# A selective scan beside a GpSimd read-out: the read of a state waits for the next drive, and other VectorE work stands between scan and drive

## The reference

```python
x = x + attn_a(layernorm(x))   # linear attention: 16 heads of 8, features poly * exp of a projection, causal
x = x + ffn(layernorm(x))      # gate/up/down, 128 -> 352 -> 128, inputs and weights rounded to FP4 in blocks of 16
x = x + attn_b(layernorm(x))   # selective state-space mixer, below
x = x + ffn(layernorm(x))
```

```python
dA  = exp(dt[..., None] * A)                      # decay
dBu = (dt * u)[..., None] * B[:, :, None, :]      # drive
h   = dA_t * h + dBu_t                            # scan over the tokens
y   = einsum('bldn,bln->bld', hs, C) + u * D      # read-out: the state times C, summed over the 16 states
```

## Time and profile before

| | before |
|---|---|
| median of 3 runs | 1835.58 us (1835.45 to 1837.35) |
| the profiled execution | 1833.05 us |
| its span in the trace | 1831.2 us |
| mean granted TensorE clock | 0.809 |
| VectorE busy | 1478.3 us, 81% |
| TensorE matmul busy | 1198.0 us, 65% |
| ScalarE busy | 669.5 us, 37% |
| GpSimd busy | 644.6 us, 35% |
| DMA | 74.75 MB, mean 41 GB/s |

### The profile page before, as it was taken

The page is one execution under the profiler, slowest core; times in us unless marked ns, Lnnn a source line. Parts: engine busy times, 40 slices in busy tenths (PEclk is TensorE's granted clock), DMA queues, the critical chain, the costliest instruction groups (busy, mean ns, idle before and its releaser), DMA issues. The chain is left out here.

```text
span 1831.2 us, 14294 instructions
## 1 busy us (share of the span) xinstructions
PE 1198.0 (65%) x4361; PEld 659.3 (36%) x4361; DVE 1478.3 (81%) x1759; ACT 669.5 (37%) x1133; POOL 644.6 (35%) x420
## 2 busy tenths in 40 slices
PE   4967964786647864688647865478745884444554
PEld 1634522454224532355214542245422552221212
DVE  1745599887998789887998879987898879975974
ACT  2524532353324523264324533245232642223211
POOL 2012244423354133432444233541344223352531
PEclk9977977898769986799778987699877997775756
DMA  2000112010210111001210102101110011102210
GB/s 55 1 6 1 48 66 78 1 47 31 75 46 1 48 58 58 35 1 54 75 69 1 48 30 74 46 1 48 52 58 34 1 54 69 69 0 70 81 40 6
DMA packets 31405, 74.75 MB, mean 41 GB/s; under 512 B 4505, under 2 KB 14562, under 8 KB 31330
## 3 DMA queue, kind: packets, MB, share of 16 engines
q1 hardware_dynamic: 31330, 73.83, 11.7%
HBM read 71.20 MB, written 2.62 MB: 40 GB/s over the span
## 5 line engine op out<-in xcount | busy, mean ns | idle before, releaser
L554 POOL TENSOR_TENSOR read<-state,bc_row 128x1024 f32<-128x1024 f32 x128 | 316.3, 2471 | 457.9 <-DVE state L1022 443.6
L1011 DVE TENSOR_TENSOR bank<-dtu,bc_row 128x1024 f32<-128x1024 f32 x128 | 383.6, 2997 | 32.1 <-POOL dtu L634 19.6
L1289 PE MATMUL bank<-read,ident 128*128 128x512 f32 x512 | 330.2, 786 | 97.1 <-POOL read L554 97.1
L671 ACT ACTIVATE decay<-dt,neg_a 128x510 f32<-128x510 f32 x256 | 169.5, 711 | 353.4 <-DVE state L1022 352.3
L1022 DVE TENSOR_TENSOR_SCAN state<-decay,bank 128x1024 f32<-128x1024 f32 x128 | 291.5, 2277 | 4.2 <-ACT decay L671 0.5
L1289 PEld LDWEIGHTS bank<-read,ident 128*128 128x128 f32 x512 | 119.6, 251 | 244.4 <-POOL read L554 123.8
L1259 PE MATMUL bank<-s_sb,vext 128*72 128x256 f32 x512 | 168.3, 412 | 0.0
L1032 DVE TENSOR_TENSOR s_sb<-bank,causal 128x512 f32<-128x512 f32 x128 | 87.9, 687 | 94.1 <-PE bank L1242 93.3
L1240 PE MATMUL bank<-feat 64*128 64x256 f32 x512 | 109.8, 463 | 80.2 <-ACT s_sb L682 79.9
L1229 PE MATMUL bank<-znt,omega 128*128 128x512 f32 x256 | 141.2, 634 | 21.7 <-ACT sqf L662 21.6
L659 ACT ACTIVATE expf<-bank,minus_s,root2s 128x512 f32<-128x512 f32 x128 | 100.2, 783 | 129.0 <-PE bank L1229 128.7
(11 more groups left out here) (220 smaller groups left out, 2011.6 us busy)
## 6 DMA issues: line engine op xcount, KB each, us to landing
bc_row<-bc_rows SPq DMA_DIRECT2D x128, 512.0 KB, 3.6
xa<-x_dram SPq DMA_DIRECT2D x8, 256.0 KB, 2.8
out_dram<-x SPq DMA_DIRECT2D x8, 256.0 KB, 2.3
omega<-omega_t_dram SPq DMA_DIRECT2D x1, 512.0 KB
bc_rows<-xdbl SPq DMA_DIRECT2D x8, 64.0 KB
wqkv<-w_qkv_t_dram SPq DMA_DIRECT2D x1, 192.0 KB
state<-w_down_dram SPq DMA_DIRECT2D x1, 176.0 KB, 2.4
state<-w_gate_dram SPq DMA_DIRECT2D x1, 128.0 KB, 2.0
```

The costliest lines, as they stand in the source:

```text
L554: pool.tensor_tensor(read[:, s % STATE_BUFFERS], state[:, s % STATE_BUFFERS], bc_row[:, s % BC_BUFFERS, 1].unsqueeze(1).broadcast_to([P, D ...
L671: last = act.activation(decay[:, s % 2, k, :, 1:], dt[:, k].rearrange("p (b t) -> p b t", b=SEQS)[:, :, 1:], ACT.Exp, scale=neg_a[:, k, s: ...
L1011: dve.tensor_tensor(bank[:, DRIVE_BANK:DRIVE_BANK + DT], dtu[:], bc_row[:, s % BC_BUFFERS, 0].unsqueeze(1).broadcast_to([P, DT, TOK]), ALU ...
L1289: last = pe.matmul(bank[:, 6 + k], ident[:], read[:, s % STATE_BUFFERS, k], start=(s == 0), stop=(s == STATES - 1))
```

## The change

There are three edits. GpSimd's read_out(k) gets a second wait: for drive k+1 (in the last slot for all drives of the group). GpSimd's slot has `attention_rest(k)` ahead of read_out(k) instead of behind it. VectorE's slot is scan(k), `attention_rest(k)`, drive(k+1).

```diff
@@ read_out (GpSimd)
                 pool.wait_ge(state_done.sem, state_done.at(group, s + 1))
 
+                pool.wait_ge(drive_done.sem, drive_done.at(group, min(s + 2, STATES)))
+
                 pool.wait_ge(y_ps.sem, y_ps.at(group, max(s + 1 - STATE_BUFFERS, 0)))
@@ body (GpSimd)
                 for k in range(SLOTS):
+                    attention_rest(turn, k)
                     if turn.has_old:
                         read_out(turn.old, k)
-                    attention_rest(turn, k)
@@ body (VectorE)
                     if turn.has_old:
                         scan(turn.old, k)
-                        if k + 1 < SLOTS:
-                            drive(turn.old, k + 1)
                     if turn.has_mid and k == 0:
                         attention_out(turn.mid, SEQS - 1)
                     attention_rest(turn, k)
+                    if turn.has_old and k + 1 < SLOTS:
+                        drive(turn.old, k + 1)
```

## The result

| | before | after |
|---|---|---|
| median | 1835.69 us (1835.45 to 1837.35, 4 runs) | 1710.20 us (1709.62 to 1718.48, 4 runs) |
| the profiled execution | 1833.05 us | 1709.62 us |
| its span | 1831.2 us | 1707.8 us |
| mean granted TensorE clock | 0.809 | 0.835 |
| VectorE busy | 1478.3 us | 1269.0 us |

The ratio is 0.9325, with a 95% interval of 0.9296 to 0.9354: 125 us faster. The forecast was 1722 us, with a range of 1680 to 1765.

What follows compares the result with a forecast made beforehand. VectorE was taken to bound the scan stage. Six turns gaining 13.1 us each (78.6), turn 8 14.9 and turn 9 19.9 sum to 113.4 off 1833.05: 1719.6, with 2.5 for the median 1722 us, range 1680 to 1765.

Steps and rivals of the forecast that it cites:

- (a): VectorE's drives in the scan stage: most fall to 1.22 us, two still wait at 1.73; 26.8 us gained a turn.
- (b): Normalisations of slots 1 and 3 stand for late reads, plus some seven other tails of 0.1: 3.0 us lost a turn.
- (c): Slots 8 to 10: Newton steps between read(8) and read(9) delay VectorE 1.8 us where 1.27 is today; 0.5 lost.
- (d): Slot 14: VectorE waits for a down-projection queued on TensorE behind sum(12), whose read ends later; 5.1 us lost a turn.
- (e): End of scan stage: read(15) comes behind norm_o's rstd, its sum runs slower; 5.1 us lost, between 3.2 and 5.5.
- TensorE's queue matters less: Rival, chance 0.13: the slot 14 loss and 1.9 us of the boundary loss go; 1671 us, half of it 1696.
- more places wait: Rival, chance 0.13: other TensorE queue positions come late, or GpSimd wins the port against drives; about 40 us more, 1762.
- The bound only changes its name: Rival, chance 0.03: saved drive time comes back as waits for decay or for a bc_row; 1835 us.
- Scan and read exclude each other: Rival, chance 0.04, the slower case: every scan of 15 waits 2.26 us for the read beside it; 1934 us.

## Why the prediction was right, point by point

The total was put 12 us too high. The mechanism held, and so did each of the places; the sizes:

**(a) Drives: right.** Forecast 26.8 us a turn. Twelve drives went from 3.41 to about 1.23 and two from 2.00 to 1.60 (forecast 1.73): 27.0. The open question, a drive 0.16 us ahead of scale_hidden, came out as taken: the first keeps what both need, drive 1.23, L539 2.59. Had it gone the other way, 27 us would have been lost by the forecast's own estimate; of the rows before the change, a single one, of another pair of instructions, spoke for this side. The two halves tried alone and the drive in SBUF show that the cause is the one named: the collision, and a scan that doesn't take part in it because one input lies in PSUM.

**(b) Tails: too high.** Forecast 3.0 lost. The normalisations of slots 1 and 3 took 2.01 and 2.99 where they took 1.10 and 2.05: 1.9. The seven tails of 0.1 don't show; slots with work gain the same 2.2 us as the bare one. This is the larger part of the 1.0 us by which the mean stage, 95.3 us, is shorter than forecast.

**(c) Slots 8 to 10: right.** Forecast 0.5 lost, slot 10 lost 0.4; VectorE waits 1.67 before qk (forecast 1.8) and qk takes 3.42. Undoing it gave 8 us in all.

**(d) Slot 14: right.** Forecast 5.1. The wait before L992 grew by 85.1 - 41.9 = 43.2 us, 5.4 for each of eight turns (in turn 9 it is in slot 8). It varies from turn to turn: slot 14 takes 8.7 to 10.1 in turns 2 to 7. In turn 4, the longest of them, the down-projection too ran at the low clock, 2.67 us where the forecast had 1.5. The turned queue took 32 us of it away.

**(e) The boundary: right in size.** Forecast 5.1, the rest grew by 5.2 in the mean, and the first mask comes 12.6 us behind the last scan instead of 7.4, also 5.2. The order of GpSimd undone brought it back to where it was, though the rest became only 1.6 us shorter, because of the new loss at the end of the stage. By parts in turn 4: the read ends 5.46 us behind the scan (forecast 5.6), the sum takes 3.31 (forecast 3.6), the projection 1.43 instead of 1.02. In turn 8 it cost 2.7, not 4.0.

**The sum.** Six turns gained 14.0 each (forecast 13.1), turn 8 16.1 (14.9), turn 9 20.1 (19.9); that is 7 of the 10 us by which the gain in the span, 123.4, exceeds 113.4. The other 2.8 lie behind turn 9's last scan, which the forecast left alone: 57.6 us before, 54.8 after, with the same work at a granted clock of 0.71 instead of 0.62. The last 2 us are the median's: after's lies 0.6 above its profiled execution, not 2.5.

**The rivals.** *TensorE's queue matters less* and *more places wait* are out: the waits are in the two places named, and near their forecast size. *The bound only changes its name* is out: decay makes a scan wait 0.5 us in all. *Scan and read exclude each other* is out for this kernel, and true of one whose drive lies in SBUF.

## What to carry to other kernels

When two engines stand in each other's way, look for the instruction of the one that the other does not disturb, here a scan with an input in PSUM, and use a semaphore to tie the disturbing instruction to it; check that other work doesn't stand between the wait and that cover, since the wait without the moved drive gave less than half. Then go through every queue past which the delayed instruction's result was moved: two waits of 5 us a turn came from queue positions on TensorE and GpSimd, and turning these two and a third, the Newton steps, gave 52 us more. Look also at the stages behind the one that became shorter: the last read, put first, gave its 5 us at its own place, and in five of six turns of the profile 3.3 of them were lost again at the end of the next stage, at TensorE's low clock.

## What the hardware showed that was not expected

Who pays in a collision is decided by a lead as small as 0.02 to 0.16 us: the read 0.02 us ahead of a drive makes the drive pay; with both inputs in SBUF the scan 0.05 us ahead of a read holds on, and the read takes 4.39 us instead of 2.34; the drive 0.16 us ahead of L539 likewise; the read 0.08 us ahead of qk makes qk pay.

TensorE's granted clock did not follow from the work nearby. In one execution, after the same idle stretch of 7 us and with the same instructions, it was back at 2.4 GHz about 5 us after the restart in one turn and still at 1.2 GHz after 10.9 us in another. With idle matmuls it held over that gap in turns 2 to 4; at the next, of 2.47 us, it was lost in turn 4 and held in turns 2 and 3. The Trainium skill, TensorE: Matmul & The Clock Gate, Part 1, lets the array rise again once it has been busy; the stretch of 10.9 us with 10.4 us busy, at 0.50, does not fit that simple reading. Why the levels fall as they do stays open; no run here settles it.
